# Second FFN layer one tile further behind the first, x loaded one tile less ahead, and new start-up orders in a cross-attention and FFN kernel on one core

## The chip, the cores and the metric

The kernel runs on one core of a Trainium2 chip. The metric is the device time of one execution in microseconds (us), the median of several runs. A smaller time is better.

## The reference

`x` is (4, 2048, 512), the context (4, 154, 512), all float32. Cut to what matters:

```python
q = layernorm(x) @ Wq; k, v = split(context @ Wkv)       # 16 heads of 64
mask = (arange(n_kv)[None] % n_q) == arange(n_q)[:, None]
x = x + softmax(where(mask, q @ k.T * 64**-0.5, -max)) @ v @ Wout + bout
h = layernorm(layernorm(x), gamma, beta)
h = gelu(qlinear(h, w1, b1)); x = x + qlinear(h, w2, b2)

def qlinear(x, w, b):
    sx = 127 / clip(max|x| over the row, 1e-5); xq = clip(round(x * sx), -128, 127)
    sw = 1 / clip(mean|w|, 1e-5);               wq = clip(round(w * sw), -1, 1)
    return xq @ wq.T / (sx * sw) + b
```

There are more queries (2048) than keys (154), so the mask leaves a query below 154 one key only, its own, and a query from 154 on none: its softmax is uniform. The attention result is therefore a row of `context @ Wv @ Wout + bout` for the first 154 rows of a batch and one mean row for the other 1894, and no query or key is computed.

## The kernel before, in words

**Tiles.** The 8192 rows of x are 64 tiles of 128 rows, rotated by two tiles on the host. Each tile t passes through: the add of its attention row (GpSimd, `add_attention`), `statistics` and `centre` (VectorE), `inverse_std` (GpSimd), `times_std` (ScalarE), `add_beta` (GpSimd), `x_scale` (VectorE, the row maximum), `round_x` (ScalarE), `widen_x` and `scale_rows` (GpSimd), `transpose_x` (a DMA transpose on SyncE's queue), `bias` (4 matmuls) and `first_layer` (2 halves of 8 matmuls, TensorE), `gelu` (2 halves, ScalarE), `half_scale` and `hidden_scale` (VectorE, the maxima of the hidden row), `round_h` (ScalarE), `transpose_h` (DMA), `widen_h` (one half on VectorE, one on ScalarE), `second_layer` (16 matmuls), `result` (VectorE) and `store`.

**What sets the order.** Nothing is scheduled automatically. Each engine has one program, written out by hand, and semaphores join them. For the first tiles (the ramp) each engine's calls are listed one by one; from step s = 6 on there is a loop over s on each engine. On TensorE a step is `bias(s)`, `first_layer(s, 0)`, `first_layer(s, 1)`, `second_layer(s - LAG)` with LAG = 3, so the second layer of a tile comes three tiles after its first. VectorE's step begins with `widen_h(s - 2)`, `result(s - LAG - 1)`; ScalarE's is `round_h(s - 1)`, `gelu(s, 0)`, `widen_h(s - 2)`, `gelu(s, 1)`, then x work of later tiles; SyncE's is `store(s - LAG - 1)`, `transpose_h(s - 1)`, `load_x(s + 11)`.

**Waits that matter.** `bias(t)` waits for `gelu(t - 1, 1)`, since the first layer's PSUM tile `p1` has one buffer. `hid`, the hidden row, has two, so `gelu(t, 0)` waits for `round_h(t - 2)`. `round_h(t)` waits for `hidden_scale(t)`. `transpose_h(t)` waits for both halves of `widen_h(t - 2)`, since `hT8` has two buffers. `widen_h(t)` waits for `second_layer(t - 2)`. x has 16 buffers, so `load_x(t)` waits for the store of tile t - 16.

**The start.** Before the first tile the kernel forms Wv @ Wout (TensorE, `products`, 32 float32 matmuls over eight chunks m, each of one Wv and one Wout load of 256 KB, into `wvo`), and the mean attention row of batch 0: `context_mean` (TensorE) gives the column means of the context, `mean_product` and `mean_weighted` (VectorE) with `mean_sum` (ScalarE) weight the rows of each chunk, and `mean_row` (one TensorE matmul after the first 14 products, then a VectorE add) makes the row that every early tile adds. Then come the sums of |w1| and |w2| (`abs_w1`, `abs_w2`, `weight_sum`, `weight_total`, `weight_scale`), the rounding of w1 (`round_w1` on VectorE, `round_weights` on ScalarE, `clip` on VectorE), the rows of attention (`out_rows`, `attn_rows`, `tail_product`, `tail_rows_out`) and the first tiles. Wout's chunks are issued from ScalarE's queue, everything else from SyncE's (`SPq` in the profile):

```python
load_ctx_b0(); load_b1()
sp.dma_start(gamma_b[:, :], gamma.partition_broadcast(P))
load_wv(0) ... load_wv(7); load_x(0); load_w1(0)
```

Of the kernel before, what the change touches and what calls it, by code (L numbers as in the profile page):

```python
# [27 lines left out]
LAG = 3  # L28
# [5 lines left out]
def block_program(nc, x, ctxm_d, ctxt_d, wvT, wout_d, bout, w1T, b1, w2T, b2, gamma, beta, ctx_b0, out, tail_rows, b1_pieces):  # L34
    es = ExitStack()
    with es:
# [149 lines left out]
        def _(sp):  # L186
# [23 lines left out]
            def load_ctx_b0():  # L210
                sp.dma_start(ctx_rows, ctx_b0[0:P, :]).then_inc(ctx_b0_loaded, 16)
                sp.dma_start(ctx_end, ctx_b0[P:KV, :]).then_inc(ctx_b0_loaded, 16)

# [61 lines left out]
            load_x(0)  # L275
            load_w1(0)
            load_w1(1)
            sp.dma_start(bout_b[:, :], bout.partition_broadcast(P)).then_inc(bout_loaded, 16)
            load_x(1)
            load_x(2)  # L280
# [3 lines left out]
            load_x(3)  # L284
            sp.dma_start(beta_b[:, :], beta.partition_broadcast(P)).then_inc(beta_loaded, 16)
            load_w1(4)
            load_w1(5)
            load_x(4)
            load_x(5)
            load_x(6)  # L290
# [6 lines left out]
            transpose_x(0)  # L297
            load_w2(2)
            load_w2(3)
            load_w2(4)  # L300
            load_w2(5)
            load_w2(6)
            load_w2(7)
# [3 lines left out]
            sp.dma_start(b2_b[:, 0, :], b2.partition_broadcast(P)).then_inc(b2_loaded, 16)  # L307
            load_x(10)
            transpose_x(1)
            load_x(11)  # L310
            load_x(12)
            load_x(13)
            transpose_x(2)
            transpose_x(3)
            transpose_x(4)
            transpose_h(0)
            transpose_x(5)
            load_x(14)
            transpose_h(1)
            load_x(15)  # L320
            transpose_h(2)
            sp.wait_ge(tail_copied, 1)
            sp.dma_start(tail_rows, tail_out).then_inc(tail_stored, 16)
            store(0)
            transpose_x(6)
            transpose_x(7)
            transpose_h(3)
            load_x(16)
            transpose_h(4)
# [3 lines left out]
            store(1)  # L333

            for s in range(6, T + LAG + 2):
                if s % 2 == 1:
                    for t in (s + 1, s + 2):
                        if live(t):
                            transpose_x(t)
                if live(s - LAG - 1):  # L340
                    store(s - LAG - 1)
                if live(s - 1):
                    transpose_h(s - 1)
                if live(s + 11):
                    load_x(s + 11)
                if s in (6, 7, 8):
                    spread_tail((s - 4) % B)
# [5 lines left out]
        def _(pool):  # L353
# [91 lines left out]
            inverse_std(1, 1)  # L445
            pool.wait_ge(beta_loaded, 16)
            add_beta(0, 1)
            inverse_std(2, 2)
            add_attention(4, 1)
            add_beta(1, 1)  # L450
            add_attention(5, 1)
# [3 lines left out]
            add_beta(2, 1)  # L455
            add_beta(3, 1)
            inverse_std(4, 2)
            scale_rows(1, 1)
            add_attention(6, 1)
            widen_x(1, 1)  # L460
            add_beta(4, 1)
            add_beta(5, 1)
            scale_rows(2, 2)
            widen_x(2, 2)
            add_attention(7, 1)
            add_attention(8, 1)
            scale_rows(4, 2)
# [3 lines left out]
            inverse_std(6, 2)  # L471
            add_attention(10, 1)
            add_attention(11, 1)
            widen_x(4, 2)
            add_b2(1)
            add_b2(2)
            add_b2(3)
            add_beta(6, 1)
            add_beta(7, 1)
# [3 lines left out]
            inverse_std(8, 2)  # L483
            inverse_std(10, 2)
            scale_rows(6, 2)
            widen_x(6, 2)
            hidden_deq(2)
            add_b2(4)
            add_attention(12, 1)
            add_beta(8, 1)  # L490
            add_beta(9, 1)
            add_b2(5)
            add_b2(6)
            add_b2(7)
            add_attention(13, 1)
            hidden_deq(3)

            for s in range(6, T + LAG):
                if live(s - 2):
                    hidden_deq(s - 2)  # L500
# [20 lines left out]
        def _(act):  # L521
            for m in range(KI):
# [82 lines left out]
            abs_w1(1)  # L605
            copy_wvo(0)
            abs_w1(2)
            copy_wvo(1)
            abs_w1(3)
            times_std(0)  # L610
            abs_w1(5)
            copy_wvo(2)
            times_std(1)
            abs_w1(6)
            abs_w1(7)
            round_x(0)
            times_std(2)
            times_std(3)
            abs_w2(0)
            copy_wvo(3)  # L620
            round_weights(0, 1)
            round_weights(0, 3)
            abs_w2(1)
            times_std(4)
            times_std(5)
            round_x(1)
            abs_w2(2)
            abs_w2(4)
            abs_w2(3)
            abs_w2(5)  # L630
# [3 lines left out]
            round_x(2)  # L634
            gelu(0, 1)
            round_x(3)
            round_weights(1, 0)
            round_weights(1, 1)
            round_x(4)
            round_x(5)  # L640
            gelu(1, 0)
            gelu(1, 1)
            round_h(0)
            round_weights(1, 2)
            round_weights(1, 3)
            round_weights(1, 4)
            gelu(2, 0)
            times_std(6)
            gelu(2, 1)
            round_h(1)  # L650
            times_std(7)
            gelu(3, 0)
            gelu(3, 1)
            round_weights(1, 5)
            widen_h(0)
            round_weights(1, 6)
            round_weights(1, 7)
            round_h(2)
            widen_h(1)
# [15 lines left out]
            for s in range(6, T + LAG):  # L675
# [4 lines left out]
                if live(s - 2):  # L680
                    widen_h(s - 2)
# [449 lines left out]
```

## Time and profile before

| | |
|---|---|
| median of 3 runs | 541.96 us (541.22 to 542.7) |
| the profiled execution: its time | 543.86 us |
| its span | 542.0 us |
| busy: TensorE / VectorE / ScalarE / GpSimd | 521.8 / 452.4 / 436.8 / 408.4 us |
| granted TensorE clock, mean | 0.993 |
| moved by DMA | 78.72 MB, mean 145 GB/s |
| chain that ended last | TensorE 77%, VectorE 3%, issue 2%, ScalarE 1%, DMA 1% of the span |

The profile is that of one execution. Its span runs from the first to the last instruction; 1.86 us of its time lie outside. "Busy" of TensorE counts pipelined matmuls, so that consecutive ones overlap by about 0.16 us. In the rows, PE is TensorE's matmuls, PEld its weight loads, DVE VectorE, ACT ScalarE, POOL GpSimd, and SPq and ACTq the DMA issues of two queues. Each float32 matmul has two records. A row of the timeline is start, duration, engine, line, operation, output and inputs, count, and in square brackets how long the engine had been idle just before and for whom.

### The profile page before, as it was taken

Reading aid. Unit: us, or ns where it says so; the run is one execution under the profiler, and the core shown is the slowest. Engines: PE = TensorE matmul, PEld = TensorE weight load, DVE = VectorE, ACT = ScalarE, POOL = GpSimd, SP = SyncE. Lnnn points to the kernel's source line nnn. Section 1 sums busy time; section 2 is a strip of 40 time slices with the busy share of each in tenths; the row PEclk is TensorE's granted clock in tenths of the full one; section 3 lists DMA queues with packets and bytes.
Section 4 is the critical chain, followed back from the end, with each engine's and each line's share of the span. In section 5 each row is a group of like instructions: output and inputs, shape, how many; then the busy total and the mean of one; then the engine's idle time right before and its main releaser. Section 6 shows DMA issues by size and latency. Waiting matters only on the chain.

```text
span 542.0 us, 8082 instructions
## 1 busy us (share of the span) xinstructions
PE 521.8 (96%) x2387; PEld 226.6 (42%) x2434; DVE 452.4 (83%) x758; ACT 436.8 (81%) x444; POOL 408.4 (75%) x533
## 2 busy tenths in 40 slices
PE   6999789799999999999999999999999999999997
PEld 3443334344444444444444444444444444444443
DVE  1799998999998888888888888889888889877653
ACT  1478988878888888888888888888888888887762
POOL 2099796988998888888898888888888889863300
PEclk8999999999999999999999999999999999999999
DMA  7996834486555545555665446556555554534433
GB/s 271 400 343 217 221 76 106 131 205 161 141 141 142 122 124 120 129 132 138 142 139 125 123 121 142 141 109 138 118 131 132 138 142 103 103 70 98 102 77 97
DMA packets 137014, 78.72 MB, mean 145 GB/s; under 512 B 114245, under 2 KB 114309, under 8 KB 136971
## 3 DMA queue, kind: packets, MB, share of 16 engines
q1 hardware_dynamic: 135819, 76.12, 55.4%
q10 hardware_dynamic: 1152, 2.10, 1.1%
q8 instruction: 19, 0.31, 0.2%
q14 instruction: 24, 0.20, 0.1%
HBM read 33.88 MB, written 17.05 MB: 94 GB/s over the span
## 4 chain that ended last, share of the span: by engine, by line
PE 77%; DVE 3%; issue 2%; ACT 1%; DMA 1%; DVEq 0%; ACTq 0%
PE py L1049 37%; PE p L1034 36%; PE p L1024 3%; DVE hmax L811 1%; DMA hT<-hq 1%; DVE hx L788 1%; DVE hid L805 0%; ACT hid L574 0%; ACT hq L583 0%; DVE xr L834 0%; DVE stat L780 0%; DVE xmax L793 0%; ACT hqT L592 0%; DVE hqT L825 0%; DVE hstep L814 0%
## 5 line engine op out<-in xcount | busy, mean ns | idle before, releaser
L1034 PE MATMUL p<-w1q,xqT 128*128 128x512 bf16 x995 | 229.1, 380 | 3.7 <-issue 1.6
L1049 PE MATMUL py<-w2q,hqT 128*128 128x512 bf16 x1006 | 229.9, 379 | 1.9 <-DVE hqT L825 1.0
L574 ACT ACTIVATE hid<-p,xdeq 128x1024 f32<-128x1024 f32 x128 | 141.8, 1108 | 27.1 <-PE p L1034 17.5
L583 ACT ACTIVATE hq<-hid,hscale 128x2048 int8<-128x2048 f32 x64 | 128.1, 2002 | 42.9 <-DVE hscale L817 42.9
L1049 PEld LDWEIGHTS py<-w2q,hqT 128*128 128x128 bf16 x1024 | 100.1, 98 | 122.1 <-DVE hqT L825 1.5
L1034 PEld LDWEIGHTS p<-w1q,xqT 128*128 128x128 bf16 x1024 | 94.8, 98 | 122.1 <-issue 14.3
L385 POOL TENSOR_TENSOR xr<-xr,attn 128x512 f32<-128x512 f32 x64 | 83.3, 1321 | 19.1 <-DVE attn L723 19.1
L811 DVE TENSOR_REDUCE hmax<-hid 128x1 f32<-128x1025 f32 x64 | 78.1, 1220 | 21.1 <-ACT hid L574 20.7
L400 POOL TENSOR_TENSOR hx<-hx,beta_b 128x512 f32<-128x512 f32 x64 | 91.9, 1456 | 2.0 <-ACT hx L559 2.0
L404 POOL TENSOR_TENSOR xr<-xr,b_b 128x512 f32<-128x512 f32 x64 | 93.0, 1474 | 0.0
L805 DVE TENSOR_REDUCE hid<-hid 128x1 f32<-128x1024 f32 x64 | 77.4, 1210 | 8.9 <-ACT hid L574 8.9
L825 DVE CAST hqT<-hT 128x1024 bf16<-128x1024 int8 x64 | 58.5, 917 | 25.0 <-PE py L1049 17.4
L431 POOL CAST xq<-xq 128x1024 bf16<-128x1024 int16 (+1 forms) x33 | 34.8, 1055 | 47.8 <-ACT xq L565 47.8
L592 ACT ACTIVATE hqT<-hT 128x1024 bf16<-128x1024 int8 x64 | 67.0, 1047 | 2.4 <-DMA hT<-hq 2.3
L788 DVE SCALAR_TENSOR_TENSOR hx<-xr,mv,gamma_b 128x512 f32<-128x512 f32 x64 | 55.4, 870 | 0.1
L834 DVE SCALAR_TENSOR_TENSOR xr<-py,hdeq,xr 128x512 f32<-128x512 f32 x64 | 47.3, 739 | 3.3 <-PE py L1049 3.3
L559 ACT ACTIVATE hx<-hx,rstd 128x512 f32<-128x512 f32 x64 | 42.8, 715 | 3.8 <-POOL rstd L392 3.2
L780 DVE BATCH_NORM_STATS2 stat<-xr 128x6 f32<-128x512 f32 x64 | 43.0, 671 | 2.0 <-POOL xr L385 2.0
L565 ACT ACTIVATE xq<-hx,xscale 128x512 int16<-128x512 f32 x64 | 42.6, 715 | 0.0
L793 DVE TENSOR_REDUCE xmax<-hx 128x2 f32<-128x1024 f32 (+1 forms) x33 | 38.6, 1171 | 0.0
L435 POOL TENSOR_TENSOR hdeq<-hstep,wmean 128x1 f32<-128x1 f32 x64 | 23.9, 376 | 17.7 <-DVE hstep L814 17.7
L979 PE MATMUL p<-wout,hid 128*128 128x512 f32 x64 | 30.2, 630 | 4.0 <-DMA hid<-wvT 4.0
(86 smaller groups left out, 293.1 us busy)
## 6 DMA issues: line engine op xcount, KB each, us to landing
xr<-x SPq DMA_DIRECT2D x64, 256.0 KB, 2.9
out<-xr SPq DMA_DIRECT2D x64, 256.0 KB, 2.4
raw<-w1T SPq DMA_DIRECT2D x8, 512.0 KB, 11.3
wout<-wout_d ACTq DMA_DIRECT2D x8, 256.0 KB, 8.2
hid<-wvT SPq DMA_DIRECT2D x8, 256.0 KB, 10.0
wout<-w2T SPq DMA_DIRECT2D x3, 512.0 KB, 8.2
xr<-w2T SPq DMA_DIRECT2D x2, 512.0 KB, 6.4
attn<-ctxm_d SPq DMA_DIRECT2D x4, 256.0 KB, 8.5
```

The costliest lines, as they stand in the source:

```text
L385: pool.tensor_tensor(xtile(t, n), xtile(t, n), a, ALU.add).then_inc(x1_ready, n)
L400: pool.tensor_tensor(htile(t, n), htile(t, n), bb, ALU.add).then_inc(xnormed, n)
L404: pool.tensor_tensor(xtile(t), xtile(t), b2_b[:, :, :], ALU.add).then_inc(xb_ready, 1)
L574: nc.scalar.activation(hid[:, t % 2, h * HALF:(h + 1) * HALF], p1[:, h * HALF:(h + 1) * HALF], ACT.Gelu, scale=col(xdeq, t)).then_inc(gelu ...
L583: nc.scalar.activation(hq8[:, t % 2, :], hid[:, t % 2, 0:HID], ACT.Copy, scale=col(hscale, t))\
L592: nc.scalar.activation(hqT[:, t % 2, NJ // 2:, :, :], hT8[:, t % 2, HALF:].rearrange("p (j t e) -> p j e t", e=2, t=P), ACT.Copy).then_inc ...
L788: nc.vector.scalar_tensor_tensor(htile(t)[:, 0, :], xtile(t)[:, 0, :], mv[:, t % 8, 0:1], gamma_b[:, :], ALU.subtract, ALU.mult).then_inc( ...
L805: nc.vector.tensor_reduce(hid[:, t % 2, HID:HID + 1], hid[:, t % 2, 0:HALF], AX.X, ALU.max, apply_absolute_value=True).then_inc(hmax_half, 1)
L811: nc.vector.tensor_reduce(col(hmax, t), hid[:, t % 2, HALF:HID + 1], AX.X, ALU.max, apply_absolute_value=True).then_inc(hmax_done, 1)
L825: nc.vector.tensor_copy(hqT[:, t % 2, 0:NJ // 2, :, :], hT8[:, t % 2, 0:HALF].rearrange("p (j t e) -> p j e t", e=2, t=P))\
L1034: mm = nc.tensor.matmul(p1[:, n * D:(n + 1) * D], xT[:, k, :], w1q[:, k, n * D:(n + 1) * D], start=False, stop=(k == KD - 1))
L1049: mm = nc.tensor.matmul(py[:, t % 2, :], hqT[:, t % 2, c // 2, c % 2, :], w2q[:, c, :], start=(c == 0), stop=(c == 2 * NJ - 1))
```

## The change

`LAG` goes from 3 to 4. In the loops, which now begin at s = 8, `widen_h` and `hidden_deq` go from s - 2 to s - 3 and `load_x` from s + 11 to s + 10. The two loads of the context of batch 0 go from SyncE's queue to the head of ScalarE's, gamma goes behind the Wv chunks and four x tiles, and the listed orders of all engines up to the loop are new. No operation is added or taken away.

```diff
-LAG = 3
+LAG = 4
@@ block.sync
-            load_ctx_b0()
             load_b1()
-            sp.dma_start(gamma_b[:, :], gamma.partition_broadcast(P)).then_inc(gamma_loaded, 16)
             load_wv(0)
...
             load_x(0)
+            load_x(1)
+            sp.dma_start(bout_b[:, :], bout.partition_broadcast(P)).then_inc(bout_loaded, 16)
             load_w1(0)
+            load_x(2)
+            load_x(3)
+            sp.dma_start(gamma_b[:, :], gamma.partition_broadcast(P)).then_inc(gamma_loaded, 16)
...
-            for s in range(6, T + LAG + 2):
+            load_x(16)
+            load_x(17)
+            transpose_x(7)
...
+            for s in range(8, T + LAG + 2):
...
-                if live(s + 11):
-                    load_x(s + 11)
+                if live(s + 10):
+                    load_x(s + 10)
@@ block.scalar
+            act.dma_start(ctx_rows, ctx_b0[0:P, :]).then_inc(ctx_b0_loaded, 16)
+            act.dma_start(ctx_end, ctx_b0[P:KV, :]).then_inc(ctx_b0_loaded, 16)
             for m in range(KI):
...
+            for s in range(8, T + LAG):
                 if live(s - 1):
                     round_h(s - 1)
                 if live(s):
                     gelu(s, 0)
-                if live(s - 2):
-                    widen_h(s - 2)
+                if live(s - 3):
+                    widen_h(s - 3)
@@ block.vector (the same move of widen_h, and of hidden_deq on block.gpsimd)
@@ block.tensor
-            products(14, 30)
+            products(14, 32)
             weight_total(0)
-            products(30, 32)
...
             weight_total(1)
+            tail_product()
             bias(1)
```

**SyncE's queue at its start.** Before:

```order
L211 DMA hx<-ctx_b0 128x512
L212 DMA hx<-ctx_b0 26x512
L221 DMA xq<-b1 16x128
L266 DMA gamma_b<-gamma 128x512
L195 DMA hid<-wvT 128x512 x8
L192 DMA xr<-x 128x512
L199 DMA raw1<-w1T 128x1024 x2
```

And of the change:

```order
L217 DMA xq<-b1 16x128
L195 DMA hid<-wvT 128x512 x8
L192 DMA xr<-x 128x512 x2
L271 DMA bout_b<-bout 128x512
L199 DMA raw1<-w1T 128x1024
L192 DMA xr<-x 128x512 x2
L275 DMA gamma_b<-gamma 128x512
```

The context (308 KB) and gamma (256 KB) no longer stand ahead of the eight Wv chunks (`hid<-wvT`).

**ScalarE's program at its start**, of the change; before, the first two rows were not there:

```order
L535 DMA hx<-ctx_b0 128x512
L536 DMA hx<-ctx_b0 26x512
L538 DMA wout<-wout_d 128x512 x8
L542 ACT_TABLE_LOAD
L542 ACTIVATE wpart<-neg_half 128x2
```

The context now stands ahead of Wout's chunks on ScalarE's queue.

**TensorE around the first second layer** (`p1<-b1rows` is a bias, `p1<-w1q` a first layer, `py<-w2q` a second). Before, from `first_layer(3)`:

```order
L1034 MATMUL p1<-w1q,xqT 128x512 x16
L1024 MATMUL p1<-b1rows,xqT 128x512 x4
L1034 MATMUL p1<-w1q,xqT 128x512 x16
L1049 MATMUL py<-w2q,hqT 128x512 x32
L1024 MATMUL p1<-b1rows,xqT 128x512 x4
L1034 MATMUL p1<-w1q,xqT 128x512 x8
L1049 MATMUL py<-w2q,hqT 128x512 x16
L1034 MATMUL p1<-w1q,xqT 128x512 x8
L1024 MATMUL p1<-b1rows,xqT 128x512 x4
L1034 MATMUL p1<-w1q,xqT 128x512 x16
```

Of the change, from `second_layer(3)` to `second_layer(4)`:

```order
L1086 MATMUL py<-w2q,hqT 128x512 x16
L1061 MATMUL p1<-b1rows,xqT 128x512 x4
L1071 MATMUL p1<-w1q,xqT 128x512 x16
L1061 MATMUL p1<-b1rows,xqT 128x512 x4
L1071 MATMUL p1<-w1q,xqT 128x512 x16
L1086 MATMUL py<-w2q,hqT 128x512 x16
```

Before, three second layers are done when the sixth first layer ends. Now `second_layer(3)` is followed by the first layers 7 and 8 with nothing between, and from there on each first layer is followed by the second layer of four tiles earlier.

## Rows read from the trace of the kernel before

**Rows 1.** Waits of TensorE after 118 us: for whom, us in total, times, longest

```profile
PE p L1034 <- issue: 1.3, 8, 0.2
```

**Rows 2.** TensorE's timeline, first and last layers

```profile
117.18 0.40 PE L1024 MATMUL p<-b1rows,xqT 32*128 32x512 bf16 x4 [0.21 <-ACT hid L574]
...
124.62 0.40 PE L1024 MATMUL p<-b1rows,xqT 32*128 32x512 bf16 x4
...
524.77 13.98 PE L1049 MATMUL py<-w2q,hqT 128*128 128x512 bf16 x62
```

**Rows 3.** TensorE's timeline, the start up to the first layer of tile 0

```profile
11.17 14.36 PE L979 MATMUL p<-wout,hid 128*128 128x512 f32 x28 [4.00 <-DMA hid<-wvT]
25.37 1.02 PE L986 MATMUL py<-xr,hT 128*128 128x512 f32 x2
26.23 13.90 PE L979 MATMUL p<-wout,hid 128*128 128x512 f32 x32
40.38 0.35 PE L991 MATMUL py<-wsum,hT 128*128 128x1 f32 x2 [0.26 <-DVE wsum L754]
...
54.88 0.81 PE L1034 MATMUL p<-w1q,xqT 128*128 128x512 bf16 x3 [0.54 <-DVE w1q L775]
```

**Rows 4.** Stretches: length, busy and instructions by engine, granted clock, DMA share, GB/s

```profile
4.90:9.70 4.80, 2.26 (x4) 0.68 (x4) 0.69 (x1) 1.49 (x2) 2.54 (x5) 0.88 0.72 251
9.70:11.10 1.40, 0.00 (x0) 0.00 (x0) 0.00 (x0) 0.00 (x0) 0.00 (x0) 0.50 1.05 405
11.10:16.50 5.40, 5.33 (x8) 2.38 (x9) 3.23 (x6) 2.74 (x8) 0.00 (x0) 0.60 1.06 393
```

**Rows 5.** DMA issues at 1.7:1.9, 2.1:2.2 and 2.6:2.7; last number: us to landing

```profile
wout<-wout_d ACTq DMA_DIRECT2D x1, 256.0 KB, 6.2
...
gamma_b<-gamma SPq DMA_DIRECT2D x1, 256.0 KB, 7.7
...
hid<-wvT SPq DMA_DIRECT2D x1, 256.0 KB, 8.6
```

**Rows 6.** VectorE's timeline: end of the mean row, weight scale, rounding of w1

```profile
21.06 3.39 DVE L717 SCALAR_TENSOR_TENSOR xr<-wout,attn,xr 128x512 f32<-128x512 f32 x4
26.50 0.69 DVE L723 TENSOR_TENSOR attn<-py,bout_b 128x512 f32<-128x512 f32 x1 [2.04 <-PE py L986]
...
41.14 0.16 DVE L761 RECIPROCAL wscale<-wmean 128x1 f32<-128x1 f32 x1
...
49.68 3.24 DVE L765 TENSOR_SCALAR w1q<-raw,wscale 128x2048 int16<-128x2048 f32 x2
```

**Rows 7.** Waits of TensorE from 26 to 118 us

```profile
PE p L1024 <- ACT hid L574: 3.2, 3, 1.7
PE p L1024 <- DMA xqT<-xq: 1.8, 1, 1.8
PE p L1034 <- DVE w1q L775: 1.2, 2, 0.6
PE py L1049 <- DVE hqT L825: 1.0, 1, 1.0
```

**Rows 8.** The stretch from 54 to 118 us, columns as in rows 4

```profile
54.00:118.00 64.00, 56.20 (x256) 23.90 (x262) 60.82 (x102) 57.63 (x61) 53.19 (x67) 1.00 0.59 146
```

**Rows 9.** VectorE's groups from 118 to 520 us: count, busy us, mean ns, idle before

```profile
L825 DVE CAST hqT<-hT 128x1024 bf16<-128x1024 int8 x55 | 49.9, 907 | 19.6 <-PE py L1049 16.6 <-DMA hT<-hq 2.8
L834 DVE SCALAR_TENSOR_TENSOR xr<-py,hdeq,xr 128x512 f32<-128x512 f32 x55 | 40.6, 738 | 0.0
```

**Rows 10.** ScalarE's timeline in step 8

```profile
119.52 2.00 ACT L583 ACTIVATE hq<-hid,hscale 128x2048 int8<-128x2048 f32 x1 [1.27 <-DVE hscale L817]
...
123.37 1.10 ACT L574 ACTIVATE hid<-p,xdeq 128x1024 f32<-128x1024 f32 x1
```

**Rows 11.** Timelines of SyncE and ScalarE in the last full step

```profile
522.98 1.29 SPq L261 DMA_TRANSPOSE hT<-hq x1
...
524.34 1.05 ACT L592 ACTIVATE hqT<-hT 128x1024 bf16<-128x1024 int8 x1
```

More of the change, by code:

```diff
@@ L302, in _ @@
             load_w2(6)
+            sp.dma_start(b2_b[:, 0, :], b2.partition_broadcast(P)).then_inc(b2_loaded, 16)
+            load_x(6)
             load_w2(7)
@@ L313, in _ @@
             transpose_x(2)
+            load_x(14)
             transpose_x(3)
+            load_x(15)
+            transpose_h(0)
             transpose_x(4)
-            transpose_h(0)
             transpose_x(5)
-            load_x(14)
             transpose_h(1)
-            load_x(15)
             transpose_h(2)
@@ L323, in _ @@
             sp.dma_start(tail_rows, tail_out).then_inc(tail_stored, 16)
+            transpose_x(6)
             store(0)
-            transpose_x(6)
-            transpose_x(7)
+            store(1)
             transpose_h(3)
-            load_x(16)
-            transpose_h(4)
             sp.wait_ge(tail_stored, 16)
@@ L332, in _ @@
             spread_tail(1)
-            store(1)
-            for s in range(6, T + LAG + 2):
+            load_x(16)
+            load_x(17)
+            transpose_x(7)
+            transpose_x(8)
+            store(2)
+            transpose_h(4)
+            transpose_x(9)
+            transpose_h(5)
+            spread_tail(2)
+            transpose_h(6)
+            spread_tail(3)
+            for s in range(8, T + LAG + 2):
                 if s % 2 == 1:
@@ L894, in _ @@
             weight_scale(1)
-            x_scale(4, 2)
             half_scale(0)
             statistics(6)
+            hidden_scale(0)
+            centre(6)
+            tail_rows_out()
+            attn_rows(1)
+            attn_rows(2)
             statistics(7)
-            hidden_scale(0)
-            half_scale(1)
             statistics(8)
             statistics(9)
+            statistics(10)
+            half_scale(1)
+            centre(7)
             hidden_scale(1)
-            centre(6)
-            centre(7)
-            half_scale(2)
+            centre(8)
+            centre(9)
             attn_rows(3)
-            statistics(10)
-            centre(8)
-            tail_rows_out()
             statistics(11)
-            hidden_scale(2)
+            widen_h(0)
             clip(1, 0)
@@ L918, in _ @@
             clip(1, 5)
-            widen_h(0)
-            widen_h(1)
             clip(1, 6)
             clip(1, 7)
+            widen_h(1)
+            half_scale(2)
+            hidden_scale(2)
             half_scale(3)
+            statistics(12)
             x_scale(6, 2)
-            centre(9)
+            hidden_scale(3)
+            x_scale(8, 2)
+            widen_h(2)
             result(0)
+            result(1)
             half_scale(4)
-            widen_h(2)
-            hidden_scale(3)
+            half_scale(5)
             hidden_scale(4)
-            result(1)
+            hidden_scale(5)
+            statistics(13)
+            widen_h(3)
+            result(2)
             centre(10)
             centre(11)
-            half_scale(5)
-            x_scale(8, 2)
-            hidden_scale(5)
-            widen_h(3)
-            for s in range(6, T + LAG + 1):
-                if live(s - 2):
-                    widen_h(s - 2)
+            half_scale(6)
+            centre(12)
+            hidden_scale(6)
+            centre(13)
+            half_scale(7)
+            hidden_scale(7)
+            widen_h(4)
+            x_scale(10, 2)
+            for s in range(8, T + LAG + 1):
+                if live(s - 3):
+                    widen_h(s - 3)
                 if live(s - LAG - 1):
@@ L1074, in _ @@
             first_layer(2, 1)
-            tail_product()
+            out_rows(3)
             bias(3)
@@ L1086, in _ @@
             first_layer(5, 0)
+            first_layer(5, 1)
             second_layer(2)
-            first_layer(5, 1)
-            for s in range(6, T + LAG):
+            bias(6)
+            first_layer(6, 0)
+            first_layer(6, 1)
+            second_layer(3)
+            bias(7)
+            first_layer(7, 0)
+            first_layer(7, 1)
+            for s in range(8, T + LAG):
                 if live(s):
```

183 lines of the change are left out of this document (96 added, 87 removed).

## The prediction

> **What bounds the kernel now.** I read the waits of TensorE first, late part before early. After 118 us TensorE waits 1.3 us in all, and for no other engine [rows 1]. A step takes 124.62 - 117.18 = 7.44 us there [rows 2], and that is bias, first and second layer back to back. So from step 8 on the time is TensorE's work, which the change leaves as it is. The end has no wait either: after the last first layer, the second layers stand in one run of 13.98 us [rows 2]. With a lag of four that run holds one more second layer and is one longer, and the work before it one shorter: zero in the sum. Only what stands before about 120 us can change.
>
> There the timeline of TensorE shows two parts. At the start it stands still for 4.00 us before its first product [rows 3], and the stretches show that its clock then falls: the granted share is 0.88 from 4.9 to 9.7 us, 0.50 (1.2 GHz) from 9.7 to 11.1 and 0.60 from 11.1 to 16.5 [rows 4]. The first 28 product records take 14.36 us, the next 32 only 13.90 [rows 3]. At the second rate 28 cost 28 x 13.90 / 32 = 12.16, so the low clock cost 2.2 us. In the ramp, TensorE's waits are listed by releaser [rows 7], 7.2 us in the four rows; VectorE is busy 60.82 of the 64 us from 54 to 118, more than TensorE (56.20) or ScalarE (57.63) [rows 8]. The ramp is VectorE's.
>
> **Part 1: the start.** Ahead of the first Wv chunk SyncE's queue carries 308 KB of context, 8 KB of b1 and 256 KB of gamma; the chunk lands at 2.6 + 8.6 = 11.2 us, gamma at 2.1 + 7.7 = 9.8 [rows 5]. Now only b1 stands ahead of it. Its partner, Wout's chunk 0, has 308 KB ahead instead, 564 KB with itself. The nearest rows on both sides: Wout's third chunk, 768 KB deep on that queue, landed at 1.7 + 6.2 = 7.9 [rows 5]; the context, 308 KB deep, had landed by 4.9, since the context mean that reads it makes up TensorE's 2.26 us of the stretch from 4.9 [rows 4] and ends at 7.17. Between them, 564 KB give 4.9 + 256 / 460 x 3.0 = 6.6, which I take, with 4.9 and 7.9 as the ends. TensorE is busy until 11.17 - 4.00 = 7.17 [rows 3], after chunk 0's 6.6, so the wait of 4.00 goes and the clock has no reason to fall. The products then need chunk m at 7.2 + 1.74m, and the queues bring one per 512 KB at about 400 GB/s [rows 4], every 1.3 us: the late end costs 0.7 us once.
>
> The 14 products end at 7.2 + 12.2 = 19.4. The mean row is next in line, and it is bound by VectorE: its last four weighting steps (3.39 us, L717) end at 24.45 [rows 6]. Chunk 7 should land at 6.6 + 7 x 1.3 = 15.7, at the late end 17; one product of 0.7 and three weightings follow, so 18.5 to 20. I take 20.1 for TensorE's mean row against 25.37 [rows 3], so 0.7 us is waited there. The 18 other products now run before the weight total: 20.1 + 1.0 + 18 x 0.87 = 36.7, against 40.38 [rows 3]. VectorE's wscale follows at 37.4 instead of 41.3 [rows 6], only 3.9 earlier. But from there to the rounding of w1 VectorE took 49.68 - 41.3 = 8.4 us [rows 6], with statistics(5) and centre(5) (about 2.9 us with the wait for tile 5) inside, which the new order puts ahead of wscale. That leaves 5.7: rounding at 43.1. The 5.2 us from there to the first layer of tile 0 (54.88 [rows 3] less 49.68) stay. **First layer at 48.3, 6.6 us earlier.** Bounds: only the mean row's shift less its wait, 5.2 (VectorE filled as before), and 7.3 (chunks early, no wait).
>
> **Part 2: the ramp.** By TensorE's waits alone [rows 7] the new order looks good. `tail_product`, now ahead of `bias(1)`, fills part of the 1.8 us for `xqT`, and I leave 1.4 since it waits for VectorE's means; the 3.2 us behind gelu occur where two first layers are adjacent, which now happens twice, 1.1 us each; the 1.0 for `widen_h` goes, since `second_layer(3)` stands one tile later; the 1.2 for w1q stays. So 7.2 falls to about 1.4 + 2.2 + 0 + 1.2 = 4.8, a further 2.4 saved.
>
> VectorE allows less. What ties it to TensorE in the loop is `hidden_scale(s-1)`, `round_h(s-1)`, `gelu(s,0)`, `widen_h`, `gelu(s,1)`, `bias(s+1)`. In step 8 round_h starts at 119.52, 2.3 us after the step, and gelu's second half ends at 124.47, 0.15 before the next bias [rows 2, 10]. That is as late as it may be. **The lag does not loosen this chain**, since `hid` still has two buffers. Moving to lag 4, at the same step TensorE has one second layer fewer behind it and so 3.45 us (13.98 / 4.05) more before it; VectorE has one widen_h (0.91) and one result (0.74) fewer done, 1.65 [rows 9]. With VectorE full, step 9 can therefore come only 1.65 us earlier than under lag 3 while 3.45 more remain: the lag **costs 1.8**. Against that stands VectorE's idle time, 64 - 60.82 = 3.2 us [rows 8]; the new order pulls x work into such holes and puts `half_scale(5)` before `hidden_scale(4)`. I cannot see how much it fills: at least 0, at most 3.2; I take the middle, 1.6.
>
> **Part 3: x ten tiles ahead, and SyncE's queue.** In the loop `load_x` waits for a store one step back, as before; its tile is added three steps later, 22 us. `transpose_h(s-1)` now waits for `widen_h(s-3)` of the same step: ScalarE's half ends at 525.39, where SyncE had issued the transpose at 522.98 [rows 11]. So SyncE runs 2.4 us later in each step, and its result is now needed a step (7.4 us) later. Cost 0; the cover is the 22 us and that step.
>
> **The sum.** -6.6 (start) +1.8 (lag) -1.6 (holes filled) = -6.4. The profiled execution, 543.86 us with a span of 542.0, would take 537.5 with a span of 535.6. The median of the runs is 541.96, 1.9 below the profiled time, so the prediction is **535.6 us**. By the bounds: -5.2 + 1.8 = -3.4 gives 538.6; -7.3 + 1.8 - 3.2 = -8.7 gives 533.3.
>
> **Rivals.**
> 1. *The start moves by bytes only.* DMA moved 251 GB/s from 4.9 to 9.7, against 405 after [rows 4]. If that dip is not gamma's doing, only its 256 KB go, on a queue that gets half: 2 x 256 / 405 = 1.3 us. TensorE still stands for 2.7 us and the clock still falls. Start -1.3, lag and holes +0.2: **540.9**. For it: the dip spans Wout's loads too. Against: Wout's third chunk, 768 KB deep, landed before gamma, 572 KB deep [rows 5]. 0.14. The Trainium skill (DMA: Bandwidth & Descriptors, "Issuing engines are not separate DMA queues") speaks for it: DMAs of all issuing engines interleave on the same 16 engines, so moving the context to ScalarE's queue saves no transfer time. The trace agrees in so far as both queues move on together at about 400 GB/s once they are full.
> 2. *VectorE is not the bound*, and TensorE's own list decides: -6.6 - 2.4, **533.0**. For it: TensorE's waits name VectorE for only 2.2 us [rows 7]. Against: rows 8. 0.16.
> 3. *The gain is lost in the ramp.* `transpose_x(7)` now stands behind `load_x(16)` and `load_x(17)`, which wait for the first two stores. By my count those come near 88 us and tile 7's transpose lands near 95, needed near 99. If results slip by more than 4 us plus the gain, TensorE waits for it: **542.0**. 0.06.
> 4. *Slower.* If SyncE's 2.4 us per step push the transposes of x past the step that needs them, every second step waits. Queued behind are `load_x` and two transposes of 1.2 to 1.3 us issue each; I find some 4 us left, so it decides only from there. Half a microsecond in each of 28 pairs is 14: 535.6 + 14 = **549.6**. 0.04.
>
> **How the numbers follow.** The forecast has 0.60, the rivals 0.14, 0.16, 0.06 and 0.04. A measurement of this kernel can tell 0.3%, 1.6 us, from no change. Faster: the forecast, rival 2 and 0.09 of rival 1, for starts between its 540.9 and the forecast, since the border is at 541.96 - 1.6 = 540.3: 0.85. Same: the other 0.05 of rival 1 and rival 3: 0.11. Slower: 0.04. The range must leave out no more than 2 in 10: it takes in rival 2's 533.0 with a little below and the late bound 538.6 with part of the way to rival 1: 532.5 to 539.5.
>
> **What would show it.** Right: TensorE's first product near 7.2 with a granted clock near 1.0 from 5 to 16 us; mean row near 20; first layer of tile 0 at 47.6 to 49.7; VectorE over 96% busy from there to step 9; TensorE's waits in the ramp 5 to 7 us, for gelu above all; after it none. Wrong: a first product after 9 us (rival 1); a wait on `xqT` in the loop (rival 4) or at tile 7 (rival 3); waits of TensorE below 5 us with VectorE under 94% (rival 2).

## The result: half a per cent slower, and the profile after

The changed kernel took 545.42 us in the median of 20 runs (542.77 to 547.05), the kernel before beside it 542.4 us (540.28 to 544.89): a ratio of 1.0051, 95% interval 1.0036 to 1.0065, so slower by about 2.8 us. The forecast was 535.6 us with a range of 532.5 to 539.5. It failed in size and in sign.

The profiled execution took 547.05 us, 1.6 above the median, with a span of 545.3. It is the longest of the 20, with a mean granted clock of 0.987 where most of them have 0.990 to 0.994, so what follows shows somewhat more of the low clock than a usual run has. Its page (span; busy time and share by engine; the granted clock and TensorE's busy tenths in 40 slices):

```profile
span 545.3 us, 8129 instructions
...
PE 529.2 (97%) x2434; PEld 228.2 (42%) x2434; DVE 444.6 (82%) x758; ACT 437.6 (80%) x444; POOL 404.2 (74%) x533
...
PE   8999899969999999999999999999999999999997
...
PEclk8999799989999999999999999999999999999999
...
PE 81%; DVE 5%; POOL 4%; DMA 4%; issue 3%; SPq 1%; ACT 1%; ACTq 0%; POOLq 0%; DVEq 0%
```

The row of TensorE dips to 6 in one slice, from 109 to 123 us, and the clock in three: at the start, near 57 and near 115. In the last line, the chain that ended last, GpSimd has 4%, and one DMA of the tail's attention rows is in it. GpSimd was in no step of my sum.

TensorE's timeline at the start, to be laid beside [rows 3]:

```profile
7.97 13.98 PE L1016 MATMUL p<-wout,hid 128*128 128x512 f32 x28 [1.00 <-DMA wout<-wout_d]
21.78 1.02 PE L1023 MATMUL py<-xr,hT 128*128 128x512 f32 x2
22.64 15.61 PE L1016 MATMUL p<-wout,hid 128*128 128x512 f32 x36
38.50 0.35 PE L1028 MATMUL py<-wsum,hT 128*128 128x1 f32 x2 [0.24 <-DVE wsum L780]
...
50.49 3.62 PE L1071 MATMUL p<-w1q,xqT 128*128 128x512 bf16 x16
56.49 0.56 PE L1028 MATMUL py<-wsum,hT 128*128 128x1 f32 x2 [2.38 <-DVE wsum L780]
```

The first product comes at 7.97 instead of 11.17, its wait is 1.00 instead of 4.00, and the first layer of tile 0 comes at 50.49 instead of 54.88: 4.4 us earlier. The stretches (columns as in [rows 4]) show that the clock fell all the same:

```profile
4.90:9.70 4.80, 3.80 (x7) 1.12 (x6) 1.83 (x3) 2.21 (x4) 0.59 (x1) 0.89 0.95 332
...
9.00:12.00 3.00, 3.00 (x5) 1.25 (x4) 1.81 (x4) 1.78 (x6) 0.00 (x0) 0.50 1.05 405
...
54.00:118.00 64.00, 54.80 (x234) 22.66 (x234) 50.40 (x91) 53.31 (x53) 45.73 (x60) 0.92 0.55 125
```

The last row answers to [rows 8]: all four engines are less busy in the ramp than before, VectorE by 10 us. Something stops them all (the longer lag alone does not: in experiment 7 VectorE is busy 62.09 of the 64 us). TensorE's waits from 26 to 118 us:

```profile
PE p L1061 <- ACT hid L589: 6.6, 2, 5.3
PE py L1028 <- DVE wsum L780: 2.6, 2, 2.4
```

One wait of 5.3 us, for gelu, before `bias(8)` (the other of the two, 1.3 us, is at 69.11, between two first layers that stand next to each other); one of 2.4 us for the weight sums. TensorE's timeline around both:

```profile
57.31 6.62 PE L1049 MATMUL py<-wvo,attn 128*108 128x512 f32 x8 [0.26 <-DVE attn L763]
...
106.12 3.63 PE L1071 MATMUL p<-w1q,xqT 128*128 128x512 bf16 x16
115.01 0.62 PE L1061 MATMUL p<-b1rows,xqT 32*128 32x512 bf16 x4 [5.26 <-ACT hid L589]
115.56 4.75 PE L1071 MATMUL p<-w1q,xqT 128*128 128x512 bf16 x16
...
131.72 0.40 PE L1061 MATMUL p<-b1rows,xqT 32*128 32x512 bf16 x4 [0.62 <-ACT hid L589]
```

TensorE was ready for `bias(8)` at 115.01 - 5.26 = 109.75. Under the lag of four one second layer fewer stands ahead of it, so the time to compare with is 117.18 - 3.45 = 113.7: at 109.75 it was still 4.0 us ahead, nearly all that the start had gained. Then come 5.26 us of waiting, 4.75 - 3.63 = 1.1 of a first layer at a low clock, 0.2 of the bias, and 0.62 before step 10, 7.2 in all. -4.0 + 7.2 = +3.2, and the spans differ by 545.3 - 542.0 = 3.3. After 132 us there is no more wait, and the end is as before.

**Who holds gelu up** is read backward. ScalarE, GpSimd, and the DMA issues of SyncE, each from its timeline:

```profile
108.56 0.72 ACT L574 ACTIVATE hx<-hx,rstd 128x512 f32<-128x512 f32 x1 [5.00 <-POOL rstd L395]
109.19 1.99 ACT L598 ACTIVATE hq<-hid,hscale 128x2048 int8<-128x2048 f32 x1
...
112.76 2.10 ACT L589 ACTIVATE hid<-p,xdeq 128x1024 f32<-128x1024 f32 x2
```

```profile
103.15 2.94 POOL L388 TENSOR_TENSOR xr<-xr,attn 128x512 f32<-128x512 f32 x2 [7.02 <-DMA attn<-tail_rows]
...
107.82 0.71 POOL L395 TENSOR_TENSOR rstd<-var_e,neg_half 128x2 f32<-128x2 f32 x1
```

```profile
77.80 10.60 SPq L257 DMA_TRANSPOSE hT<-hq  x2
88.45 0.54 SPq L318 DMA_DIRECT2D tail_rows<-wout  x1
...
94.58 1.27 SPq L257 DMA_TRANSPOSE hT<-hq  x1
95.95 0.49 SPq L236 DMA_DIRECT2D attn<-tail_rows  x1
...
96.83 0.35 SPq L241 DMA_DIRECT2D attn<-tail_rows  x1
```

`bias(8)` waits for `gelu(7, 1)`. Before it in ScalarE's program stand `round_h(5)` and, first, `times_std(10)`, which idles 5.00 us for `inverse_std(10)`. That stands on GpSimd behind `add_attention(14)` and `(15)`, which sat 7.02 us for their attention rows. These rows come by `spread_tail(1)`, and SyncE issues that at 95.95 to 97.2: the store that it reads from stood behind two hidden transposes (77.80 to 88.40), and it stands itself behind a third. In the chain that ended last:

```profile
96.83 6.16 DMA attn<-tail_rows
```

Before, GpSimd added the same two tiles at 111.9, in the loop, without a wait; their rows had been issued at 101.1 to 102.3. The new lists move the add 16 us forward (GpSimd stood ready for it at 103.15 - 7.02 = 96.1), and the issue of its rows only 5.

### The profile page after: what moved, and what is told of

It reads as the page before. It is cut to its first block, busy times and chain, and to the rows that moved or that the text cites. A ratio compares the mean times of both kernels' runs of the same rounds, so it can differ in the third digit from the quotient of the medians.

```text
span 545.3 us, 8129 instructions
## 1 busy us (share of the span) xinstructions
PE 529.2 (97%) x2434; PEld 228.2 (42%) x2434; DVE 444.6 (82%) x758; ACT 437.6 (80%) x444; POOL 404.2 (74%) x533
## 4 chain that ended last, share of the span: by engine, by line
PE 81%; DVE 5%; POOL 4%; DMA 4%; issue 3%; SPq 1%; ACT 1%; ACTq 0%; POOLq 0%; DVEq 0%
PE py L1086 37%; PE p L1071 37%; PE p L1061 3%; PE p L1016 3%; POOL xr L388 2%; DMA wout<-w2T 1%; PE py L1049 1%; DMA attn<-tail_rows 1%; DMA wout<-wout_d 1%; DVE hmax L837 1%; DVE hid L831 1%; ACT hid L589 1%; DVE xmax L819 1%; POOL hx L403 1%; PE py L1041 1%
## 5 line engine op out<-in xcount | busy, mean ns | idle before, releaser
L1071 PE MATMUL p<-w1q,xqT 128*128 128x512 bf16 x1024 | 233.2, 381 | 0.0
L388 POOL TENSOR_TENSOR xr<-xr,attn 128x512 f32<-128x512 f32 x64 | 81.8, 1298 | 27.9 <-DVE attn L749 18.2
L407 POOL TENSOR_TENSOR xr<-xr,b_b 128x512 f32<-128x512 f32 x64 | 91.8, 1454 | 0.0
L851 DVE CAST hqT<-hT 128x1024 bf16<-128x1024 int8 x64 | 56.3, 879 | 23.5 <-PE py L1086 23.4
L434 POOL CAST xq<-xq 128x1024 bf16<-128x1024 int16 (+1 forms) x33 | 33.6, 1017 | 46.7 <-ACT xq L580 46.7
L814 DVE SCALAR_TENSOR_TENSOR hx<-xr,mv,gamma_b 128x512 f32<-128x512 f32 x64 | 52.7, 827 | 0.1
L1061 PE MATMUL p<-b1rows,xqT 32*128 32x512 bf16 x256 | 25.4, 388 | 7.2 <-ACT hid L589 7.2
## 6 DMA issues: line engine op xcount, KB each, us to landing
raw<-w1T SPq DMA_DIRECT2D x8, 512.0 KB, 12.2
```

The source lines that it names most:

```text
L388: pool.tensor_tensor(xtile(t, n), xtile(t, n), a, ALU.add).then_inc(x1_ready, n)
L407: pool.tensor_tensor(xtile(t), xtile(t), b2_b[:, :, :], ALU.add).then_inc(xb_ready, 1)
L814: nc.vector.scalar_tensor_tensor(htile(t)[:, 0, :], xtile(t)[:, 0, :], mv[:, t % 8, 0:1], gamma_b[:, :], ALU.subtract, ALU.mult).then_inc( ...
L851: nc.vector.tensor_copy(hqT[:, t % 2, 0:NJ // 2, :, :], hT8[:, t % 2, 0:HALF].rearrange("p (j t e) -> p j e t", e=2, t=P))\
L1071: mm = nc.tensor.matmul(p1[:, n * D:(n + 1) * D], xT[:, k, :], w1q[:, k, n * D:(n + 1) * D], start=False, stop=(k == KD - 1))
```

## The experiments

**The theory.** The two halves of the forecast are right in kind (the earlier start gains, the lag costs), and what turned the sign is the one jam above. Rivals: the lag alone costs more than the start gives; the early start itself causes the jam; the late load of w2(7) and its slow clock are the loss. Each experiment has the profile of one execution, and 6 to 12 runs timed beside the kernel before. The experiments ran on three chips, so I compare them by their ratios to before; such a ratio can differ from the quotient of the two medians by 0.1%. "About equal" below means that the intervals overlap.

**1. The tail's rows stored and spread early.**

```diff
+            sp.wait_ge(tail_copied, 1)
+            sp.dma_start(tail_rows, tail_out).then_inc(tail_stored, 16)
             transpose_x(5)
             transpose_h(1)
+            sp.wait_ge(tail_stored, 16)
+            sp.wait_ge(attn_copied, B)
+            spread_tail(1)
             transpose_h(2)
```

(and the same lines taken away further down).

> Edit: the changed kernel, with the store of the tail rows and the three DMAs of spread_tail(1) issued on SyncE ahead of transpose_h(2) instead of behind transpose_h(3). Theory A (the tail rows): TensorE's 5.3 us wait at bias(8) is GpSimd's add_attention(14) waiting for spread_tail(1), which landed at 103.0 us, with inverse_std(10), times_std(10), round_h(5) and gelu(7) in line behind it. Then the wait at bias(8) falls below 1 us, the clock does not fall after it, and the time is about 6 us below the changed kernel's, 539 (0.994 of the kernel before). Theory B (VectorE is full, as my prediction had it): another wait of about the same size takes its place, and the time stays at 544 or above.

541.22 us, ratio to before 0.9965 (0.9944 to 0.9987). GpSimd no longer waits, and `bias(8)` is early:

```profile
92.36 2.50 POOL L388 TENSOR_TENSOR xr<-xr,attn 128x512 f32<-128x512 f32 x2
```

```profile
107.29 0.40 PE L1061 MATMUL p<-b1rows,xqT 32*128 32x512 bf16 x4 [1.30 <-ACT hid L589]
...
115.58 0.40 PE L1061 MATMUL p<-b1rows,xqT 32*128 32x512 bf16 x4 [0.88 <-ACT hid L589]
...
124.87 0.40 PE L1061 MATMUL p<-b1rows,xqT 32*128 32x512 bf16 x4 [1.88 <-ACT hid L589]
```

The row at 107.29 is `bias(8)`. The same DMAs, issued some 20 us earlier, take 4.2 us off the changed kernel's median (0.86%, or 4.7 us, by the ratios) and turn it from slower than before to slightly faster. It is less than theory A said (539 us, and a wait below 1 us). Of the 5.3 us, 1.30 stay before `bias(8)`, and 0.88 + 1.88 come back before the next two biases: there the chain that ended last leads through VectorE's maxima of the hidden rows and ScalarE's gelu.

**2. The attention of tiles 14 and 15 added later.**

```diff
-            add_attention(14, 1)
-            add_attention(15, 1)
             widen_x(8, 2)
...
             inverse_std(12, 2)
+            add_attention(14, 1)
+            add_attention(15, 1)
```

> Edit: the changed kernel, with add_attention(14) and (15) on GpSimd moved four places back, behind inverse_std(12). SyncE's queue is left alone. Theory A: inverse_std(10) runs at about 97 instead of 107 us, the wait at bias(8) goes, about 539 to 541. If instead the late transposes or stores themselves hold TensorE (theory C: SyncE's queue is what is late, not the row that GpSimd adds), the wait stays and the time is 545.

540.72 us, 0.9964 (0.9941 to 0.9987), about equal to the first. GpSimd's add of the rows, and `bias(8)`:

```profile
101.18 2.95 POOL L388 TENSOR_TENSOR xr<-xr,attn 128x512 f32<-128x512 f32 x2
```

```profile
108.52 0.40 PE L1061 MATMUL p<-b1rows,xqT 32*128 32x512 bf16 x4 [1.30 <-ACT hid L589]
```

SyncE still issues the rows behind the same transposes, at 93.4 to 94.6 us, but the add has no wait, and `inverse_std(10)` runs ahead of it, at 95.5. So it is the order on GpSimd against the order on SyncE, not the lateness of either.

**3. w2's last block loaded first.**

```diff
+            load_w2(7)
             load_x(6)
-            load_w2(7)
```

(with b2's broadcast, which stood ahead of both, behind x's next loads).

> Edit: the changed kernel, with the last w2 load issued ahead of b2 and x tile 6. It landed at 55.0 us and TensorE waited 2.4 us for the weight sum behind it, after which its clock was low and tail_product took 6.6 instead of 3.6 us. Theory A says that the wait at step 8 ends by SyncE's queue (the transpose of h(2) ahead of the tail store), which itself hangs on work behind that weight sum. So TensorE's wait at 54 us falls to about 1.5, tail_product to 3.6, and the wait at bias(8) grows by nearly as much as was saved, less what moves with the chain: 543 to 545. If the early waits count in full, 540 to 541.

542.92 us, ratio 1.0 (0.9974 to 1.0025). The wait for the weight sums falls, `tail_product` runs at full clock, and the jam stays (5.01 us before `bias(8)`):

```profile
53.61 0.35 PE L1028 MATMUL py<-wsum,hT 128*128 128x1 f32 x2 [0.45 <-DVE wsum L780]
55.38 3.68 PE L1049 MATMUL py<-wvo,attn 128*108 128x512 f32 x8 [1.42 <-DVE attn L763]
```

In the changed kernel w2(7) lands 8.1 us after its issue, TensorE waits 2.38 + 0.26 us, and the same 8 matmuls take 6.62. Here the two waits are 0.45 + 1.42 and the matmuls take 3.68, together 3.7 us less. The median falls by 2.5 us (2.8 by the ratios): most of it does get through to the end, more than my theory A had (543 to 545).

**4. Both together (1 and 3).**

> Edit: the changed kernel, with the tail rows early (as in e1) and the last w2 load ahead of b2 and x tile 6 (as in e3). e3 showed TensorE ready at step 8 1.1 us earlier or more than e1, with the wait then filled by the tail rows. If the two are separate waits in a row, the fixes add: e1's 0.9965 less 0.003 to 0.004, 0.993. If VectorE's chain bounds the stretch behind, the second fix only moves the wait to gelu: 0.996.

540.46 us, 0.997 (0.995 to 0.999), about equal to the first alone, as the expectation has it where VectorE's chain bounds the stretch (0.996). The profiled execution had two low clocks that the first had not (28 product records in 13.98 us, `tail_product` in 5.38), so its times do not tell the two apart. Its `bias(10)` is of use further down:

```profile
126.38 0.40 PE L1061 MATMUL p<-b1rows,xqT 32*128 32x512 bf16 x4 [1.88 <-ACT hid L589]
126.71 3.63 PE L1071 MATMUL p<-w1q,xqT 128*128 128x512 bf16 x16
```

**5. The new start alone, on the kernel before.** The context at the head of ScalarE's queue, gamma behind x's first tile; all orders and the lag as before.

```diff
-            load_ctx_b0()
-            sp.dma_start(gamma_b[:, :], gamma.partition_broadcast(P)).then_inc(gamma_loaded, 16)
             load_x(0)
+            sp.dma_start(gamma_b[:, :], gamma.partition_broadcast(P)).then_inc(gamma_loaded, 16)
@@ block.scalar
+            act.dma_start(ctx_rows, ctx_b0[0:P, :]).then_inc(ctx_b0_loaded, 16)
+            act.dma_start(ctx_end, ctx_b0[P:KV, :]).then_inc(ctx_b0_loaded, 16)
```

> Edit: the kernel before, with only the start of the change: the context loads at the head of ScalarE's queue, gamma behind x tile 0, nothing else moved. In the changed kernel's trace the first product starts at 7.97 instead of 11.17 us and the mean row at 21.8 instead of 25.4. If the ramp of the kernel before is bound by VectorE (as predicted), everything behind the mean row moves along: 3.4 us saved, 538.6 (0.9937). If the waits behind it (weights, DMA landing) eat it, 541 to 542.

539.39 us, 0.9926 (0.9901 to 0.9951); repeated with more rounds (its expectation stands under 9), 539.63 us, 0.9933 (0.9909 to 0.9956). TensorE's start, and the stretch of [rows 4]:

```profile
7.14 12.28 PE L980 MATMUL p<-wout,hid 128*128 128x512 f32 x28
20.49 1.12 PE L987 MATMUL py<-xr,hT 128*128 128x512 f32 x2 [1.07 <-DVE xr L718]
```

```profile
4.90:9.70 4.80, 4.80 (x10) 1.54 (x9) 2.02 (x4) 2.41 (x5) 0.88 (x2) 1.00 1.05 382
```

This is the start as forecast: no wait, full clock, 12.28 for the 28 records (12.2), mean row at 20.49 (20.1). The gain that reaches the end is 3.0 us (second median against before) to 4.0 (first ratio). Its ratio is the lowest of the study: faster than before and than the change.

**6. Which of the two loads mattered.** Gamma's move alone, and the context's alone, each on the kernel before (the halves of the diff above).

> Edit: the kernel before, with only gamma's load moved behind x tile 0. Theory G (gamma's broadcast causes the slow DMA stretch from 5 to 8 us): the first product starts near 7.5 us with the wait gone or below 1 us, and the time is that of e4, 0.9926. Theory H (bytes only): the first chunk lands 1.3 us earlier, the first product at 9.9, clock low again, 0.997.

> Edit: the kernel before, with only the context's two loads moved to the head of ScalarE's queue; gamma stays ahead of the Wv chunks. Theory G: gamma's broadcast is now first in SyncE's queue, beside the context, the slow stretch is still there (earlier, from 3 us) and delays the context too: context mean later than 4.9 us, first product at 9 to 11, time 0.995 to 1.0. Theory H: Wout's chunk lands 308 KB deeper and Wv's 308 KB shallower, first product near 9, 0.996.

538.85 us, 0.995 (0.9928 to 0.9971), and 539.21 us, 0.9956 (0.9939 to 0.9973): both faster than before, and gamma's move alone about equal to both moves together. TensorE's start, first with gamma moved:

```profile
7.34 12.63 PE L979 MATMUL p<-wout,hid 128*128 128x512 f32 x28 [0.23 <-DMA hid<-wvT]
```

and with the context moved:

```profile
8.34 13.98 PE L980 MATMUL p<-wout,hid 128*128 128x512 f32 x28 [1.52 <-DMA wout<-wout_d]
```

256 KB less ahead bring the first product from 11.17 to 7.34, far more than rival 1's 1.3 us by bytes, so that rival has fallen. The stretches from 3 to 6 and from 5 to 8 us show where the slow DMA went; before:

```profile
3.00:6.00 3.00, 2.86 (x11) 1.88 (x9) 0.00 (x0) 0.02 (x1) 0.52 (x1) 1.00 0.87 279
5.00:8.00 3.00, 2.16 (x4) 0.58 (x4) 0.69 (x1) 1.49 (x2) 2.33 (x5) 1.00 0.56 190
```

with gamma moved back:

```profile
5.00:8.00 3.00, 2.77 (x6) 0.94 (x7) 0.74 (x2) 1.05 (x2) 2.28 (x5) 1.00 1.01 339
```

and with the context moved, gamma first on SyncE's queue behind b1:

```profile
3.00:6.00 3.00, 3.00 (x12) 2.18 (x11) 0.00 (x0) 0.00 (x0) 2.39 (x5) 1.00 0.88 197
5.00:8.00 3.00, 1.82 (x4) 0.29 (x2) 0.69 (x1) 1.06 (x1) 0.57 (x1) 1.00 0.90 330
```

The slow stretch goes with gamma. Moved back, it leaves 350 GB/s from 3 to 6 and 339 from 5 to 8. Issued about 0.9 us earlier, as in the last run, it brings the slow stretch forward (197 GB/s from 3 to 6), and the rate is up again once gamma has landed, 4.9 us after its issue at 1.2, at about 6 us; before, gamma landed at 9.8. That is theory G of the expectation, except that its first product, "at 9 to 11", was too late. Why the load of gamma is slow no run shows, and it is not the only cause of a low rate: the changed kernel moves 197 GB/s from 5 to 6 with gamma out of the way.

What moving the context gained is order: the product waits for the later of two chunks. Wv's chunk 0 landed at about 7 (5.3 us after an issue at 1.6 to 1.8) instead of 11.2, and Wout's at 8.34 instead of about 4.6. The Trainium skill (DMA: Bandwidth & Descriptors, "Issuing engines are not separate DMA queues") has it that DMAs run on the same 16 DMA engines and interleave whichever engine started them, so that using several issuing engines saves issue time only. The trace agrees for full queues, 405 GB/s from 9.7 to 11.1 before and 404 in the changed kernel; that section does not speak of which chunk lands first, and that is what the move changed here.

**7. The lag alone, on the kernel before.** `LAG` to 4, `widen_h` and `hidden_deq` to s - 3, `load_x` to s + 10, in the loops, and in the lists the calls that the longer lag defers taken out: one each of `second_layer`, `widen_h`, `result`, `hidden_deq`, `store` and `load_x`.

> Edit: the kernel before, with only LAG 4, widen_h and hidden_deq at s - 3, load_x at s + 10, and the entries that the longer lag defers taken out of the lists (second_layer(2), widen_h(3), result(1), hidden_deq(3), store(1), load_x(16)); start and all other orders as before. My prediction said that a longer lag costs 3.45 - 1.65 = 1.8 us when VectorE is full in the ramp, since the chain through the hidden row is not loosened: 543.8 against 542 (1.003). If instead the lag lets TensorE run ahead (the reading of its own waits), the 1.0 us wait for widen_h goes and the time falls by 1 to 3 us: 0.996.

545.68 us, 1.0078 (1.006 to 1.0096).

```profile
99.03 0.40 PE L1018 MATMUL p<-b1rows,xqT 32*128 32x512 bf16 x4 [3.80 <-ACT hid L571]
99.36 5.32 PE L1028 MATMUL p<-w1q,xqT 128*128 128x512 bf16 x16
...
115.40 0.40 PE L1018 MATMUL p<-b1rows,xqT 32*128 32x512 bf16 x4
```

The row at 115.40 is `bias(8)`, against the 113.73 that one second layer fewer would make of it: +1.7, near the forecast's 1.8, and the spans differ by 1.6. All runs together say more, +4.2 us by the ratio and +3.6 by the medians: the profiled execution of before, at 543.86, lies 1.5 above its own median of 542.4. The wait is again for gelu, and the chain of waits leads from it to VectorE's maxima of the hidden row. After it the clock is low for one first layer (5.32 instead of 3.63), which my term did not have. At `bias(6)` TensorE is 1.6 us late (99.03, against 100.86 - 3.45 = 97.41 before), then the low clock adds 1.7, and two waits of before are gone, 1.00 for `widen_h` and 0.21 at `bias(8)`. So +1.7 is a sum of more parts than mine, and that it comes near 1.8 is in part luck.

**8. Start and lag, with the old listed orders.** Edits 5 and 7 together.

> The kernel before with both the new start (context tile 0 at the head of ScalarE's queue, gamma's broadcast behind x's first tile) and the lag of four, but with the old listed orders of the ramp. Theory (the lag costs what it cost alone, 545.68 us and a ratio of 1.0078, and the new orders' gelu(7) jam behind the late attention rows is what lost the rest): the two changes add up, 0.9926 * 1.0078 = 1.0003, about 542 to 543 us; TensorE waits for hid once near 95 us for about 3.8 us at bias(6), and bias(8) follows with no wait. Rival (the jam comes from the earlier start itself, whatever the lists): add_attention(14) runs into the rows of the tail here too, TensorE waits about 5 us before bias(8), and the time is 545 us or more. Rival (the start's gain swallows the lag's wait, since ScalarE and VectorE have the earlier start too): 540 us or less.

543.04 us, 1.0014 (0.9987 to 1.004), near the product 0.993 x 1.0078 = 1.0007. There is one wait at `bias(6)` (5.20 us, where 3.8 was expected) and none at `bias(8)`:

```profile
97.39 0.61 PE L1019 MATMUL p<-b1rows,xqT 32*128 32x512 bf16 x4 [5.20 <-ACT hid L572]
97.94 4.93 PE L1029 MATMUL p<-w1q,xqT 128*128 128x512 bf16 x16
...
113.59 0.39 PE L1019 MATMUL p<-b1rows,xqT 32*128 32x512 bf16 x4
```

GpSimd adds the attention of tiles 14 and 15 without a wait:

```profile
107.65 2.51 POOL L382 TENSOR_TENSOR xr<-xr,attn 128x512 f32<-128x512 f32 x2
```

So neither the early start nor the lag jams GpSimd; the new lists do. By the medians they make 545.42 out of 543.04, but the intervals of the two ratios touch (up to 1.004 here, from 1.0036 for the change), so the size of what the lists cost as a whole is not sure.

**9. All three edits on the changed kernel (1, 2 and 3), and the start alone again.**

> The changed kernel with all three edits of its ramp: the tail's rows stored and spread early, w2(7) ahead of b2 and x(6), and the attention of tiles 14 and 15 added behind the deviation of tile 12. Theory (each jam is gone once with the first edit, and what is left is VectorE's and ScalarE's own work in the ramp): no gain over the first two together, 540 us, ratio 0.996 to 0.998. Rival (GpSimd's order still costs): bias(8) earlier than 108.8 by over 1 us, and the ratio 0.993 to 0.995.

> The kernel with the new start alone a second time, with more rounds, beside the one with the lag too. If its gain is real the ratio is again 0.990 to 0.995 (539 us). Rival: it was the luck of one chip, and the ratio lies above 0.997.

539.82 us, 0.9949 (0.9925 to 0.9972). Its interval overlaps that of experiment 4, so whether the third edit adds anything is open. Its `bias(8)` comes at 106.17, 2.6 us ahead of experiment 4's 108.81, and with that ratio both marks of the expectation's rival are met. But they prove nothing for it: the profiled execution had a full clock where that of experiment 4 had a low one, 1.0 us by the first layer of tile 0 (49.58 against 50.62) and 1.7 at `tail_product` (3.68 against 5.38), which is all of the 2.6. The first layer of tile 0 comes 5.3 us earlier than before (49.58 against 54.88):

```profile
7.89 12.28 PE L1016 MATMUL p<-wout,hid 128*128 128x512 f32 x28 [0.34 <-DMA wout<-wout_d]
```

**The account, by ratios to before.** Start -0.7% (-3.8 us), lag +0.8% (+4.3), new lists as they stand +0.4% (+2.0, not clear of noise): 1.0051. The lists freed of both jams bring -0.65% instead (0.9949 against 1.0014, -3.5 us), and then the whole is about as fast as the new start alone. The new lists with the new start and the old lag were not run. The lag earns nothing that can be seen in any of these runs.

## Why the prediction was wrong, by its steps

*Part 1, the start: right in mechanism, mis-sized.* I had -6.6; the profile shows -4.4 at the first layer of tile 0, and the new start by itself -4.8 and -4.1 there (the two profiles of experiment 5) and -3.8 at the end, by the ratios. The wait did not vanish but came to 1.00 us, for Wout's chunk, the partner now 564 KB deep: chunk 0 landed at 7.97, which is my late end of 7.9, not the 6.6 that I took. "The clock has no reason to fall" was wrong with it: 28 records took 13.98 and not 12.2. The two, 0.8 and 1.8 us, less the 0.7 of slack at the mean row, account for 1.9; the mean row came 1.7 later, at 21.78 instead of 20.1, the weight total 1.8 and the first layer 2.2. Whether Wout's chunk lands in time differs from one execution to the next. With context and gamma moved, the first product came after no wait in both profiles of experiment 5, after 0.24 to 0.65 us in experiments 1, 2, 3 and 9, each time with 28 records in 12.28 us, and after 1.00 to 1.05 in the changed kernel and experiments 4 and 8, each time with 13.98. Even in experiments 1, 2, 3 and 9 the first layer came only 5.1 to 5.3 us earlier than before, at the low end of my bounds of 5.2 to 7.3.

*Part 2, the lag: +1.8 came near in the profile (+1.7, in part by luck, see experiment 7), too small over all runs: +4.2 (experiment 7) and +4.4 (8 against the repeated 5) by the ratios, +3.6 and +3.4 by the medians.* That TensorE waits for gelu behind VectorE's maxima of the hidden row, and that a longer lag does not loosen this, is what experiment 7 shows. What I left out is the low clock for one first layer behind the long wait (5.32 us instead of 3.63, after 3.80).

*Part 2, "holes filled" at -1.6: this is the step that failed.* I priced the new lists by two engines, TensorE's waits and VectorE's idle time, and set 0 as the worst that reordering could do. The runs show +2.0 in its place (experiment 8 against the change), and -3.5 once the jams are out. GpSimd appears nowhere in it, though every tile's x passes through it twice ahead of ScalarE. The new list put `add_attention(14)` on GpSimd ahead of where SyncE's list lets its rows land, and a wait of an engine with slack became one of TensorE's: 7.02 us on GpSimd, 5.00 on ScalarE, 5.26 on TensorE. The second jam is of the same kind: w2(7) behind b2 and x(6) on SyncE's queue, 2.48 us on ScalarE, 2.38 on TensorE, 2.9 of low clock. By experiments 1 and 3 they cost 0.86% and 0.5% one by one, and 1.0% with all three edits. The sign turned here, since experiments 1 and 2 are faster than before; but the forecast would have missed without it: of the 8.9 us between the forecast's -6.4 and the +2.5 of the account, this step has 3.6, the start 2.8 and the lag 2.5.

*Part 2, TensorE's waits of 4.8 us:* near in sum once the jams are gone, less so in kind. In experiment 9 TensorE waits 3.5 us for gelu, three times (2.2 forecast), 1.42 at `tail_product` for VectorE's means (1.4 forecast), and not at all for `w1q` (1.2) or `widen_h` (0), 4.9 against 4.8. "VectorE over 96% busy" fell with the jam (50.40 of 64 us); without it, in experiment 1, it is 59.97 of 64, or 94%.

*Part 3 held:* no wait on `xqT` in the loop and none on loads of x. But my count of SyncE's queue looked at transposes of x and at loads only, and passed over the two issues that mattered.

*The rivals.* 1 fell, by experiment 6: the slow stretch was gamma's doing. 2 and 3 did not come. 4, the one on the slower side, looked for SyncE's lateness in every step of the loop; what came was SyncE's lateness once, in the ramp, at a transfer that I had not followed. Its kind was nearest, its place and price (+14) were wrong, and a chance of 0.04 on that side was far too small for a change that rewrites the ramp's order on five engines.

## What to carry to other kernels

Where a change rewrites in-order lists by hand, price each moved call against the time at which its input lands, on every engine and every queue, also those with a quarter of their time idle: an in-order engine with slack can pass one late input on to whoever stands behind (here 7.02 us on GpSimd became 5.26 on TensorE). The worst case of a reordering is not zero; it is the time from when the moved call is ready until its late input lands (here 7 us). And a wait of TensorE can cost more than its length, since the clock may be low for the work behind it (here by 1.1 us after 5.26 and by 2.9 after 2.38).

## What the runs showed that I had not expected

*A wait of TensorE is not always followed by a low clock, and its length does not decide it.* At the start, 0.23 to 0.65 us of idle time left the 28 records at 12.28 to 12.63 us, while 1.00, 1.05, 1.52 and 4.00 us of it were followed by 13.98 to 14.36. In the ramp 1.30 us before a first layer left that at 3.63, and 2.38, 3.80 and 5.26 us were followed by 6.62 (instead of 3.68), 5.32 and 4.75 (instead of 3.63). But the same 1.88 us before `bias(10)` were followed by 5.31 in experiment 1 and by 3.63 in experiment 4. What decides it no run here shows.

*The executions of one kernel differ with such falls.* Of the changed kernel's 20 runs the four with a mean granted clock of 0.994 took 542.8 to 543.9 us, the nine at 0.991 took 544.6 to 546.2, and the two at 0.987 546.6 and 547.1. The new start alone has a mean clock of 0.996 to 1.0 in all of its 18 runs, before mostly 0.993 or 0.994. A part of its gain is that its products run at 2.4 GHz from the first one on (12.28 us instead of 14.36 for the 28 records). Later its clock can fall too: both of its profiles have one first layer of 5.3 us, behind waits of 1.97 and 2.07.
